# Head stacks of 25 rows in four row groups, with both score passes interleaved on TensorE

## What is computed

```python
Q = proj(query, w_q, b_q); K = proj(key, w_k, b_k); V = proj(value, w_v, b_v)   # 16 heads of 8
Q = _apply_rope(Q, cos, sin); K = _apply_rope(K, cos, sin)
scores = jnp.einsum('bhqd,bhkd->bhqk', Q, K) / math.sqrt(DK)
scores = jnp.where(mask == 0, jnp.asarray(-1000000000.0, scores.dtype), scores)
attn = jax.nn.softmax(scores, axis=-1)
ctx = jnp.einsum('bhqk,bhkd->bhqd', attn, V)
return ctx.transpose(0, 2, 1, 3).reshape(b, -1, D) @ w_o.T + b_o
```

## Time and profile before

| | us |
|---|---|
| median of 3 runs | 344.03 |
| runs, lowest to highest | 341.42 to 351.15 |
| the profiled execution | 340.95 |
| its span, first to last instruction | 338.6 |
| TensorE busy in the span | 293.8 (87%) |
| VectorE, ScalarE, GpSimd busy | 221.0, 160.2, 156.1 |

### The profile page before, as it was taken

How to read it: one execution, slowest core, us unless ns; L and a number is a source line. 1 busy time by engine, 2 the same in 40 slices (tenths; PEclk the granted TensorE clock), 3 DMA queues, 4 the chain that set the end, 5 groups by cost and what they waited for, 6 DMA issues and landing times.

```text
span 338.6 us, 4644 instructions
## 1 busy us (share of the span) xinstructions
PE 293.8 (87%) x1570; PEld 189.8 (56%) x1570; DVE 221.0 (65%) x485; ACT 160.2 (47%) x278; POOL 156.1 (46%) x174
## 2 busy tenths in 40 slices
PE   3637899899999898898799969969998996999993
PEld 1422454354445454556577746847765674777771
DVE  4825686565778555786975774497587478666662
ACT  1110034445554576655555527735455844445541
POOL 6365033122212333294686744384655266465551
PEclk9955569999999999999999979997999999899999
DMA  7697936328401020201110100200000000001001
GB/s 211 206 130 206 195 109 185 67 77 149 90 2 51 15 64 2 62 0 20 44 39 27 62 0 0 64 0 0 0 4 0 0 2 0 0 0 33 0 2 31
DMA packets 10247, 18.17 MB, mean 54 GB/s; under 512 B 1328, under 2 KB 7024, under 8 KB 9712
## 3 DMA queue, kind: packets, MB, share of 16 engines
q1 hardware_dynamic: 8496, 11.59, 15.4%
q10 hardware_dynamic: 1728, 6.29, 6.4%
HBM read 15.19 MB, written 2.62 MB: 53 GB/s over the span
## 4 chain that ended last, share of the span: by engine, by line
PE 51%; DVE 16%; DMA 12%; POOL 7%; ACT 5%; issue 4%; SPq 4%; POOLq 0%; ACTq 0%; DVEq 0%
PE psum L1032 47%; DMA qk_scratch<-parts 6%; DMA ctxk<-ctx_tok 3%; DVE early L1002 2%; DVE xn L898 2%; DVE negmax L983 2%; DVE early L1008 2%; DMA pvT<-mask_k 2%; POOL big L546 1%; DMA big<-qk_scratch 1%; ACT early L686 1%; POOL parts L546 1%; DVE stats L727 1%; SPq L383 1%; SPq L368 1%
## 5 line engine op out<-in xcount | busy, mean ns | idle before, releaser
L1002 DVE TENSOR_TENSOR early<-early,psum 128x512 f32<-128x512 f32 x64 | 43.7, 683 | 49.2 <-ACT early L686 49.0
L686 ACT ACTIVATE early<-psum 128x512 f32<-128x512 f32 x64 | 38.3, 598 | 67.4 <-PE psum L1032 67.3
L546 POOL TENSOR_TENSOR parts<-early,parts 128x512 fp32r<-128x512 f32 x32 | 41.3, 1290 | 49.4 <-ACT parts L678 49.4
L1032 PE MATMUL psum<-xs,ws 128*128 128x512 f32 x192 | 56.5, 431 | 0.0
L1032 PE MATMUL psum<-xs,big 128*128 128x512 f32 x192 | 54.9, 422 | 0.0
L983 DVE TENSOR_REDUCE negmax<-psum 128x4 f32<-128x1024 f32 x32 | 39.1, 1222 | 23.3 <-PE psum L1032 23.2
L648 ACT ACTIVATE early<-psum 128x1024 f32<-128x1024 f32 x32 | 32.7, 1023 | 30.9 <-PE psum L1032 30.8
L1008 DVE TENSOR_TENSOR early<-early,psum 128x512 f32<-128x512 f32 x64 | 44.0, 687 | 4.3 <-POOL big L546 1.6
L1032 PE MATMUL psum<-maskb,id 128*128 128x512 bf16 x128 | 43.2, 423 | 2.0 <-DVE negmax L983 1.9
L1032 PEld LDWEIGHTS psum<-big 32*128 32x128 f32 (+1 forms) x256 | 21.0, 203 | 38.7 <-issue 29.8
L1032 PE MATMUL psum<-big 32*128 32x256 f32 (+1 forms) x256 | 35.1, 355 | 7.0 <-DMA big<-qk_scratch 6.9
(11 more groups left out here) (180 smaller groups left out, 436.1 us busy)
## 6 DMA issues: line engine op xcount, KB each, us to landing
raw<-experts ACTq DMA_DIRECT2D x12, 512.0 KB, 3.7
big<-qk_scratch SPq DMA_DIRECT2D x24, 128.0 KB
qk_scratch<-parts SPq DMA_DIRECT2D x16, 128.0 KB, 2.5
big<-qk_scratch SPq DMA_DIRECT2D x16, 64.0 KB
early<-sel SPq DMA_DIRECT2D x2, 512.0 KB, 7.7
ropet<-rope SPq DMA_DIRECT2D x2, 256.0 KB, 4.7
ctxk<-ctx_tok SPq DMA_DIRECT2D x1, 512.0 KB, 9.4
out<-x_in SPq DMA_DIRECT2D x2, 256.0 KB, 3.1
```

Of the source, the lines that this page charges most:

```text
L546: nc.gpsimd.tensor_tensor(hs(n)[:, 1, :], h32[:, n % 2, :], hs(n)[:, 0, :].bitcast(F32), ALU.subtract).then_inc(lo_ready, 1)
L686: nc.scalar.activation(sg[:, n % 2, :], psum[:, n % 2, :], ACT.Silu).then_inc(silu_ready, 1)
L1002: nc.vector.tensor_tensor(sg[:, n % 2, :], sg[:, n % 2, :], psum[:, 2 + n % 2, :], ALU.mult).then_inc(up_read, 1)
L1032: return nc.tensor.matmul(o, w, r, start=start, stop=stop, skip_group_check=True)
```

## The change

Stacks now have 24 rows for A (the product of the two low parts is left out) and 25 for B, at partitions 0, 32, 64 and 96: four heads in four row groups. Pair `i` of a batch uses groups 0 and 1 if even, 2 and 3 if odd. B_START is 7, which is odd, so A and B of one slot use different groups; their eight score matmuls stand interleaved, after all masks. There are 40 slots: 7 with A alone, 25 with both, 7 with B alone, one for the last pv.

A now has a ring of three one-bank buffers (banks 0 to 2), B has 3 and 4, pv has only bank 5. The reduce of a pair is two reduces of one bank each, and they come after VectorE's small tasks of the slot. `maxT` stands every four slots, for half a batch (four transposes); ScalarE copies its result and issues its DMA. On TensorE the small tasks stand between the two masks of A, pv after them and ahead of the masks of B. ScalarE does copies that others wait for ahead of exp, and the rest behind it. All four batches have room in `stacks`, so the reuse of a buffer needs no wait. SP's queue has 22 DMAs a batch for 14, with 0.77 MB read back for 1.0 MB; the ones of a stack come by DMA and not by GpSimd's memsets. The selectors load into `pvT` and `ctxk`, and the keys by token (`ctxk`) load after the stack of batch 2.

```diff
-LAG = 3
+HEADS = 2 * B * PAIRS
+A_RING = 3
-B_START = PAIRS + LAG
+B_START = 7
...
-        if s == PAIRS * (b + 1) - 1:
-            tasks.insert(0, ("maxT", b))
         tasks += tail_tasks(s, b)
+    if s % (PAIRS // 2) == 0 and s // (PAIRS // 2) <= 2 * B:
+        tasks.append(("maxT", s // (PAIRS // 2) - 1))
...
-        BANK_PV = 4
+        BANK_PV = 5
...
+        def a_bank(s, r):
+
+            return (2 * s + r) % A_RING
+
+        def b_bank(t, r):
+
+            return r if t + B_START >= A_SLOTS and (t + B_START - A_SLOTS) % 2 == 1 else A_RING + r
+
+        def head_rows(i, r, n):
+
+            g = 2 * (i % 2) + r
+            return slice(32 * g, 32 * g + n)
...
+                sp.wait_ge(scratch_k[b], 16)
+                for g in range(4):
+                    read_both(1, g)
                 sp.wait_ge(qks_ready, 2 * b + 2)
                 write(0, scratch_q[b])
...
+                for g in range(4):
+                    read_one(1, g, 0)
+                sp.wait_ge(scratch_q[b], 16)
+                for g in range(4):
+                    read_twice(0, g)
+                    read_one(0, g, 1)
...
+                elif name == "maxT":
+                    if b >= 2:
+                        act.wait_ge(maxrow_in[b - 2], 16)
+                    evict(task, maxrow[:, b % 2, :], m[0:4, :])
+                    act.wait_ge(misc_act, misc_reads(task))
+                    nc.scalar.dma_start(stacks[24:128:32, 0, b // 2, 2 * (b % 2):2 * (b % 2) + 2, :].bitcast(F32).rearrange("g j q -> g (j q)"),
+                                        maxrow[:, b % 2, :].bitcast(F32)).then_inc(maxrow_in[b], 16)
...
+                if s < A_SLOTS:
+
+                    b, i = s // PAIRS, s % PAIRS
+                    dve.wait_ge(scores_max, s + 1)
+                    for r in range(2):
+                        nc.vector.tensor_reduce(negmax[:, b % 2, :, i // 2, 2 * (i % 2) + r],
+                                                psum[:, a_bank(s, r), :].rearrange("p (t k) -> p t k", t=QT), AX.X,
+                                                ALU.max, negate=True).then_inc(maxes_read, 1)
...
+                def mask_a(r):
+                    if 2 * s + r >= A_RING:
+                        pe.wait_ge(maxes_read, 2 * s + r - A_RING + 1)
+                    mm(psum[:, a_bank(s, r), :], id16[:, :], maskb[:, 0, :, :].rearrange("p t k -> p (t k)"), True, False)
...
+                    mask_a(0)
+                for task in tasks:
+                    if task[0] != "maxT":
+                        misc_task(*task)
+                if has_a:
+                    mask_a(1)
+                for task in tasks:
+                    if task[0] == "maxT":
+                        misc_task(*task)
+                if t >= 2 and t % 2 == 0:
 
                     quad = t // 2 - 1
                     pb = quad // QUADS
                     pe.wait_ge(exps_done, 2 * quad + 2)
...
+                if has_b:
+
+                    if s == A_SLOTS + 1:
+                        pe.wait_ge(maxes_read, HEADS)
+                    reads = t if t >= 1 and b_bank(t - 1, 0) == b_bank(t, 0) else t - 1
+                    if reads >= 1:
+                        pe.wait_ge(exps_done, reads)
+                    for r in range(2):
+                        mm(psum[:, b_bank(t, r), :], id16[:, :], maskb[:, 1, :, :].rearrange("p k q -> p (k q)"), True, False)
...
+                for half in range(QT):
+                    if has_a:
+                        for r in range(2):
+                            last_a = scores_a(half, r)
+                    if has_b:
+                        for r in range(2):
+                            last_b = scores_b(half, r)
```

More of the change, by code:

```diff
@@ L86 @@
 MISC_READER = {
-    "xT": "act", "qproj": "dve", "kproj": "dve", "vproj": "dve", "maxT": "dve", "ctx0": "dve",
+    "xT": "act", "qproj": "dve", "kproj": "dve", "vproj": "dve", "maxT": "act", "csum": "dve", "ctx0": "dve",
     "ctx1": "dve", "ctxT": "act", "oproj": "dve", "xT2": "dve", "logits": "dve", "wT": "dve", "yT": "dve",
@@ L108, in slot_tasks @@
         tasks.append(("vproj", 1))
+    if s == PAIRS + 2:
+        tasks.append(("csum", 0))
     for b in range(B):
@@ L260, in build @@
         stack_in = [sem(f"stack_in{b}") for b in range(B)]
-        maxrow_in = [sem(f"maxrow_in{b}") for b in range(B)]
+        maxrow_in = [sem(f"maxrow_in{b}_{i}") for b in range(B) for i in range(2)]
         out_done = sem("out_done")
@@ L379, in read_turned, with rows_of @@
-                def read_turned(r):
-                    src = qk_scratch[b, r, 0].rearrange("l (d j) q -> l d (j q)", j=PAIRS)
-                    for half in range(2):
-                        sp.dma_start(rows_of(0, r, 16)[8 * half:8 * (half + 1), :], src[1 - half]).then_inc(stack_in[b], 16)
+                    sp.dma_start(qk_scratch[b, t].rearrange("l p q -> p l q"), qks[:, b % 2, t, :, :].bitcast(F32)).then_inc(written, 16)
+                def rows_of(t, g, first, n):
+                    return stacks[32 * g + first:32 * g + first + n, t, b, :, :].bitcast(F32).rearrange("c j q -> c (j q)")
@@ L409, in _, with ones_beside_keys @@
+                sp.wait_ge(scratch_q[b], 16)
+                for g in range(4):
+                    read_twice(0, g)
+                    read_one(0, g, 1)
+            def ones_beside_keys(b):
+                for g in range(4):
+                    sp.dma_start(stacks[32 * g + 24:32 * g + 25, 1, b, :, :].bitcast(F32), ones[0:8, :]).then_inc(stack_in[b], 16)
             for s in range(SLOTS):
@@ L414, in _ @@
                             late_loads()
-                    if name == "maxT":
-                        maxrow_batch(b)
+                        if b == 2:
+                            keys_by_token()
             for g in range(GROUPS):
@@ L436, in _ @@
             pool.wait_ge(pool_consts, 1)
-            def ones_beside_keys(buffer):
-                for r in range(2):
-                    nc.gpsimd.memset(stacks[64 * r + 32:64 * r + 33, 1, buffer, :, :].bitcast(F32), 1.0).then_inc(ones_rows, 1)
-                pool.wait_ge(ones_rows, 2 * (buffer + 1))
-            ones_beside_keys(0)
             def inv_sqrt(n, at):
@@ L642, in _ @@
                 t = s - B_START
+                tasks = sorted(slot_tasks(s), key=lambda task: (task[1], task[0] != "xT")) if s == 0 else slot_tasks(s)
+                for name, b in tasks:
+                    if s == 0 or MISC_READER.get(name) == "act":
+                        misc_task(name, b)
+                if t >= 2 and t % 2 == 0:
+                    c = t // 2 - 1
+                    act.wait_ge(pv_done, c + 1)
+                    if c == 0:
+                        act.wait_ge(masks_ready, 1)
+                    elif c % QUADS == 0:
+                        act.wait_ge(misc_full, misc_index(("ctx1", c // QUADS - 1)) + 1)
+                    nc.scalar.copy(pvT[:, c % QUADS, :], psum[:, BANK_PV, 0:S]).then_inc(pv_evicted, 1)
                 if 0 <= t < A_SLOTS:
@@ L1068, in misc_task @@
                     pe.wait_ge(maxes_read, PAIRS * (b + 1))
-                    for t in range(QT):
-                        last = nc.tensor.transpose(m[0:16, P * t:P * (t + 1)], negmax[:, b % 2, t, :], id32[:, :])
+                    for j in range(2):
+                        for t in range(QT):
+                            last = nc.tensor.transpose(m[0:4, S * j + P * t:S * j + P * (t + 1)],
+                                                       negmax[:, b // 2 % 2, t, 2 * (b % 2) + j, :], id32[:, :])
+                elif name == "csum":
+                    pe.wait_ge(consts_ready, 1)
+                    last = mm(m[:, 0:E1], ones[:, :], c2[:, 1, :])
                 elif name in ("ctx0", "ctx1"):
                     t = 0 if name == "ctx0" else 1
-                    pe.wait_ge(pv_evicted, 2 * (b + 1))
+                    pe.wait_ge(pv_evicted, QUADS * (b + 1))
                     for q in range(QUADS):
```

181 lines of the change are left out of this document (60 added, 121 removed).

## The result

| | before | after |
|---|---|---|
| median, us | 344.05 | 354.67 |
| lowest to highest | 341.42 to 351.15 | 351.79 to 358.68 |
| ratio, 95% interval | | 1.033 (1.022 to 1.044) |
| profiled execution, its span | 340.95, 338.6 | 355.27, 353.4 |

The change makes the kernel slower by about 11 us. The ratio leaves out runs that are over 1.5% above the fastest of the same kernel. Two later comparisons gave ratios of 1.030 (1.023 to 1.037) and 1.037 (1.029 to 1.044).

A forecast was written before the change was run, and what follows sets the result against it. TensorE was taken to bound the attention stage. End of slot 6 at 39.9, plus 77.7 full slots, 20.9 second pass alone and 4.4 clock, put experts at 142.9, 7.5 us later: sum 348.4, given as 348, range 337 to 359.

The forecast's parts named there:

- Start: Batch 0's reads before the first scores: reads issued by about 21, first scores at 25.5 us, bounds 23 and 28.
- First-pass slots: The 7 slots of the first pass alone: 2.15 us each at 1.2 GHz, plus 0.8 for maxT, ending at 39.9.
- Clock after the start: Slots 7, 8 and 9: 2.4 GHz only after slot 9, costing 4.4 us more, bounds 0 and 10.
- Full slots: Slots 7 to 31, both passes: short 2.15, long 3.16 us, with maxT and excess 77.7 us, 3.1 a slot.
- The lump in slot 24: Full slot 24: route1 stands before ctx0 and ctx0 before maxT, 1.2 us of excess.
- ScalarE after maxT: Full slots with maxT: ScalarE's copy and DMA issue precede exp and delay it, 0.6 us in the sum.
- Eight score matmuls: Scores of both passes in a full slot: four row groups abreast, 0.43 us for eight; two abreast would take 0.87.
- Rival (c): Full slots: row groups do not run four abreast, 10.8 us more, total 359; chance 0.12.
- Second pass alone: The last 7 slots with scores, up to the experts: 20.9 us, for 22.5 before in 11 slots.
- Rival (d): After the start: the low clock lasts to slot 15, 6 us more, total 354; chance 0.18.
- The sign to look for: TensorE's timeline: waits for exp of 15 us or more in total, and value products starting 0.04 after an exp.

## Why the prediction was right and where it failed

The main reason is shown. The forecast said that the value product ahead of the masks puts it in series with exp and takes back what the lags and row groups give. Undoing this gave the time of before. It did not give less, so with the value product back in its place the lags and row groups still gave nothing over before. Four row groups measured 0.2 us a slot and the lag some 3 us, and slots with maxT and the series of exp, masks and scores in short slots use that up. The size of the loss was too small in the forecast: the median is 354.67 for 348, and the experts start at 150.0 for 142.9, 7.1 us late. That it stayed as near as this is partly luck, since 4.4 us for the clock at the start did not come and 5.6 at the end, which were not forecast, did. By the steps of the sum:

- **Start, 25.5 forecast, 27.76 measured: +2.3.** The failed step is "four key reads of 0.6 at most" and "issued by about 21". SyncE's queue in after:

```profile
13.27 2.75 SPq L388 DMA_DIRECT2D big<-qk_scratch  x4
16.07 0.45 SPq L380 DMA_DIRECT2D qk_scratch<-parts  x1
...
23.21 0.50 SPq L398 DMA_DIRECT2D big<-qk_scratch  x1
```

  A read took 0.69 us to issue, the query write went from 14.19 to 16.07, and the last read went out at 23.21. The smaller volume that I counted as a gain was no term: the issues bound the start, as the split over two queues shows (first scores at 25.35).
- **First-pass slots, 2.15 forecast, 2.13 measured** (28.48 to 32.74 for two), and maxT 1.1 more (34.14 to 37.35 from scores to scores) for the 0.8 forecast.
- **Clock after the start, 4.4 forecast, some 1.2 measured.** The clock rose at 44.7, in slot 7, and not behind slot 9. Only slot 7 was longer for it: 3.28 us from scores to scores (41.60 to 44.89) for the 2.1 of the sum. This is inside the 80.1 us of the next item. The reading that the clock of before fell while TensorE waited for the stack was off too: it fell at 18.0 us, and that wait of 6.90 us began after 20.
- **Full slots, 77.7 plus the clock forecast, 80.1 measured.** Long ones 3.20 and 2.20 for short ones, against 3.16 and 2.15; maxT slots 2.94 from scores to scores, so 0.74 for 0.73. The lump in slot 24 was right in kind and place: maxT waited 1.44 us for ctx0. What the sum had too small, beside slot 7, is ScalarE after maxT. Its copy and its DMA issue stand ahead of exp, here in slot 12:

```profile
60.38 0.58 ACT L587 CAST maxrow<-psum 4x512 fp32r<-4x512 f32 x1 [0.56 <-PE psum L1082]
...
60.98 0.52 ACTq L608 DMA_DIRECT2D big<-maxrow  x1
...
61.61 1.02 ACT L671 ACTIVATE early<-psum 128x1024 f32<-128x1024 f32 x1 [0.65 <-PE psum L1043]
```

  Exp starts 0.53 us after TensorE has left the scores (61.08) and not 0.12, and the long slot behind each maxT lasts 3.56 to 3.59 from scores to scores and not 3.20. That is 0.4 us six times, over 2 us for the 0.6 forecast.
- **Eight score matmuls, 0.43 forecast, 0.44 measured.** An estimate by the ratio of 3.07 in the Trainium skill ("TensorE: Matmul & The Clock Gate", "Measured speedup vs the span model") was 0.56; no such loss shows for these 256 columns. But the price of the opposite case was wrong: two groups take 0.68 and not 0.87. In that run the pairs start at 67.11, 67.33, 67.45 and 67.57 and the next mask at 67.79: a further pair costs 0.12 us, and the rest of the 0.43 for four matmuls is the start and end of a set, which eight pay once. Rival (c) would have been 5 us by the slots, 2.5 by the medians, and not 10.8.
- **Second pass alone, 20.9 forecast, 27.6 measured: +6.7.** This is the step that failed most. With the clock up it takes 22.1, so the slots were costed 1.2 too low (slot 32 alone 4.47 for 4.0), and 5.6 is the clock, a term that the sum did not have here. I asked after the clock at the start, where there is idle time in the first-pass slots, and not here, where VectorE's small tasks ahead of maxT and the serial exp that I had priced leave TensorE without work. Rival (d) had the mechanism and a price of 6 us, in the wrong stretch.
- **The sign to look for.** I expected 15 us or more of waits of TensorE for exp. The waits of after, between 42.3 and 150:

```profile
PE psum L1043 <- DVE negmax L1005: 7.7, 12, 1.8
PE psum L1043 <- ACT early L671: 5.0, 8, 1.1
PE psum L1082 <- DVE ctxn L840: 3.5, 3, 1.6
```

  Much of the time behind exp stands under negmax, since the second mask of the first pass breaks the wait in two: it goes at 0.86 after the scores, exp is over at 1.18. The total of the waits was badly chosen as a sign; the other one, that the value product starts 0.04 after exp, held (0.04 to 0.06).

The sum: 2.3 for the start, 2.4 for the full slots with what the clock cost them, 6.7 for the end, less the 4.4 that stood for the clock: 7.0 of the 7.1 us.

## What to carry over

In a chain of two passes, look at what runs on TensorE between the last score matmul and the end of exp: a work item that itself waits for exp gives no cover, and 1 us of it moved in front of the masks cost 0.8 us in each slot that had it and nothing else. In the kernel before, where a half of the first pass stands there too, the same move cost 0.1 us a full slot in the profile. When work moves to an engine that a chain runs through (here ScalarE's copy and DMA issue ahead of exp), price the delay each time it comes. When a change makes TensorE wait, price the clock in every stretch in which it will wait, the ones behind the main loop too. For small matmuls in row groups, take the price of a group of them from the starts of a long set, not from four times a short one.

## What the runs showed of the hardware

- Score matmuls in free row groups started ahead of earlier ones in the program (first four of the set: two of 24 rows and two of 25). Interleaving them by hand gained nothing.
- 23 matmuls of 512 columns added to a chain with waits went with 5.6 us less for it (27.7 to 22.1), as the granted clock stayed at its upper level. Without them and with the same waits the clock fell for 17 us in three profiles and stayed up longer in a fourth.
- The issue of a DMA takes time on the queue that issues it: 0.69 us for a read of the stack on SyncE's queue. With four of batch 0's 16 reads on ScalarE's queue the first scores started at 25.35 us; with all on one queue the profiles have 27.4 to 29.4.
- The granted clock of a profile can miss a fall. In the run with VectorE's order changed the first-pass slots read 1.00, and a mask there takes 0.61 us, as at the lower level, and 0.39 at the upper. The timeline of that kernel:

```profile
29.75 0.61 PE L1048 MATMUL psum<-maskb,id 128*128 128x512 bf16 x1
30.60 0.61 PE L1048 MATMUL psum<-maskb,id 128*128 128x512 bf16 x1 [0.25 <-DVE negmax L978]
```

  The pace of the matmuls is the safer sign of the two.
